# Spreading the last batch's row scatters, fillers, blankings and routing over the blocks of two expert mixtures

## The reference

```python
x = x + 0.5 * ffn(layernorm(x))
x = x + attention(layernorm(x))       # 16 heads of 8, q = k = v
x = x + 0.5 * ffn(layernorm(x))       # the same weights

# ffn: rows are normalised again (gain and bias), a router picks 2 of 8 experts
logits = xf @ router_w
scores, idx = top_k(logits, 2); gate = softmax(scores)
# each expert: layernorm, x1 = x @ W1 + b1 (512 wide), x2 = clip(x @ W2 + b2, -20, 20)
#   hidden = clip(x1 * silu(x2)); y = clip(hidden @ Wo + bo)
out = sum over the experts of gate * y
```

## Time and profile before

| | |
|---|---|
| median of 3 runs | 1469.3 us (1467.14 to 1470.9) |
| profiled execution | 1478.64 us, span 1476.9 us |
| PE busy | 1268.9 us (86%) |
| DVE busy | 1175.9 us (80%) |
| ACT busy | 898.2 us (61%) |
| GpSimd busy | 515.8 us (35%) |
| chain that ended last | PE 52%, DVE 24%, issue 8%, DMA 4%, SyncE's queue 4%, ACT 4% |

### The profile page before, as it was taken

How to read it: one execution, slowest core, us unless ns; L and a number is a source line. 1 busy time by engine, 2 the same in 40 slices (tenths; PEclk the granted TensorE clock), 3 DMA queues, 4 the chain that set the end, 5 groups by cost and what they waited for, 6 DMA issues and landing times.

```text
span 1476.9 us, 29483 instructions
## 1 busy us (share of the span) xinstructions
PE 1268.9 (86%) x10053; PEld 653.3 (44%) x10053; DVE 1175.9 (80%) x2341; ACT 898.2 (61%) x1882; POOL 515.8 (35%) x603
## 2 busy tenths in 40 slices
PE   3735999887789999999969999969996988799992
PEld 3634788775122223323213223213321237688881
DVE  8783888787988998888948898948897648778885
ACT  1212455554368888787748887748875864455651
POOL 3873453343432002324342433330444022433331
PEclk9999999999699999999979999979999999899996
DMA  7124454553302110021111011101100222355635
GB/s 256 41 73 155 163 189 177 223 196 100 86 14 84 35 35 26 11 84 36 27 37 35 22 37 34 42 23 35 35 4 29 78 88 104 119 185 195 237 144 181
DMA packets 65382, 135.58 MB, mean 92 GB/s; under 512 B 13330, under 2 KB 34932, under 8 KB 65204
## 3 DMA queue, kind: packets, MB, share of 16 engines
q1 hardware_dynamic: 56052, 115.39, 22.9%
q0 software_dynamic: 8704, 16.93, 3.4%
q10 hardware_dynamic: 480, 1.38, 0.3%
HBM read 47.35 MB, written 25.07 MB: 49 GB/s over the span
## 4 chain that ended last, share of the span: by engine, by line
PE 52%; DVE 24%; issue 8%; DMA 4%; SPq 4%; ACT 4%; another core or an unknown queue 2%; POOL 2%; ACTq 0%; DVEq 0%; POOLq 0%
PE psum L2188 13%; DVE att_neg_part L1874 10%; PE psum L2164 7%; PE psum L2098 6%; PE psum L2086 5%; PE psum L2088 5%; PE psum L2168 5%; PE psum L2145 5%; DVE stats L1529 2%; DMA ffn_block_rows<-rows_dram 2%; ACT att_probs L1408 1%; DVE att_neg_part L1879 1%; DVE ffn_x2c L1815 1%; DVE ffn_hidden L1826 1%
## 5 line engine op out<-in xcount | busy, mean ns | idle before, releaser
L1408 ACT ACTIVATE att_probs<-psum 128x512 f32<-128x512 f32 x1024 | 556.3, 596 | 171.1 <-PE psum L2170 104.6
L1874 DVE TENSOR_REDUCE att_neg_part<-psum 128x2 f32<-128x1024 f32 x441 | 532.0, 1222 | 91.6 <-PE psum L2146 73.2
L2188 PE MATMUL psum<-att_probs,att_values 128*16 128x256 f32 x4096 | 325.1, 390 | 7.3 <-ACT att_o_t L1423 3.9
L1375 ACT ACTIVATE ffn_silu<-ffn_x2c,ffn_rec 128x256 f32<-128x256 f32 (+1 forms) x320 | 154.6, 487 | 192.7 <-DVE ffn_x2c L1815 141.2
L1237 POOL DMA_INDIRECT y_dram<-ffn_y,ffn_block_rows x144 | 142.2, 988 | 291.1 <-ACT ffn_y L1393 262.9
L2145 PE MATMUL psum<-att_right,att_left 64*128 64x512 bf16 x512 | 200.4, 392 | 44.4 <-ACT att_probs L1408 16.5
L1815 DVE TENSOR_SCALAR ffn_x2c<-psum,ffn_rec 128x256 f32<-128x256 f32 (+1 forms) x320 | 162.5, 513 | 61.1 <-PE psum L2088 40.8
L2167 PE MATMUL psum<-att_right,att_left 64*128 64x512 bf16 x512 | 201.0, 393 | 10.6 <-DVE att_neg_part L1874 8.2
L2164 PE MATMUL psum<-att_right,att_left 64*128 64x512 bf16 x512 | 200.7, 392 | 4.4 <-DVE att_neg_part L1874 4.3
L2146 PE MATMUL psum<-att_right,att_left 64*128 64x512 bf16 x512 | 200.9, 393 | 0.0
L2168 PE MATMUL psum<-att_right,att_left 64*128 64x512 bf16 x512 | 196.1, 383 | 0.0
(11 more groups left out here) (215 smaller groups left out, 1532.3 us busy)
## 6 DMA issues: line engine op xcount, KB each, us to landing
ffn_rec<-record SPq DMA_DIRECT2D x80, 776.5 KB, 3.6
ffn_block_rows<-rows_dram SPq DMA_DIRECT2D x64, 130.0 KB
att_left<-q_parts_dram SPq DMA_DIRECT2D x64, 96.0 KB
att_right<-q_parts_dram SPq DMA_DIRECT2D x124, 48.0 KB
record<-in_L_ffn_W SPq DMA_DIRECT2D x16, 256.0 KB, 6.3
last_y<-y_dram SPq DMA_DIRECT2D x8, 512.0 KB, 7.4
att_right<-q_parts_dram SPq DMA_DIRECT2D x92, 32.0 KB
y_dram<-ffn_y,ffn_block_rows POOLq DMA_INDIRECT x144
```

The lines of the kernel that those rows point to most:

```text
L1408: S.activation(probs[:, slot % PROBS, :], ring_bank(("score", slot))[:, :], ACT.Exp, scale=SCALE).then_inc(att_bank.by_act, 1)
L1874: last = V.tensor_reduce(out=neg_part[:, h % 2, keys, p::PAIR, t], in_=psum[:, low:high + 1, :], axis=AX.X, op=ALU.max, negate=True)
L2188: last = TE.matmul(value_bank[head * VS:head * VS + VW, q], values[:, b % 2, kt, team * TEAM + head, :], probs[:, (UNIT * n + j) % PROBS, ...
```

## The change

In mixture 0 the last batch's 16 scatters go from the end of the first routing into the blocks from 3 on, alternately two and one a block. The blankings go from block 8 to block 14, and memsets are cut: values into one piece per tile, operands into pieces of 256 columns, also for the two sets blanked ahead of attention. The fillers go one a block into blocks 8 to 15 (mixture 0) and two a block into 13 to 16 (mixture 1). In mixture 1 the eight scatters of `JOBS[-2]` are spread over slots 0 to 24, those of `JOBS[-1]` over slots 36 to 52, its other steps over slots 11 to 34 in smaller parts, and the late lay-out into eight parts in slots 35 to 49 with some independent instructions no longer waiting for each other. `JOBS[-1]` becomes a GpSimd job for `xf` and its rows, and its exponential is e to the ratio as a power on GpSimd, for which DVE's gates wait. ACT runs one small Silu before each mixture.

```diff
@@ build_macaron
+    BLANK = 256
         def on_pool(job):
-            return job[0] == 1 and job[1] < B - 1
+            return job[0] == 1 and job != JOBS[-2]
@@ TAIL
-        plan_tail([0], "route", JOBS[-2], ROUTE_STEPS - 1)
+        plan_tail([0, 0, 12, 16, 16, 20, 20, 24], "route", JOBS[-2], ROUTE_STEPS - 1)
...
-        for step, slot in ((0, 10), (1, 12), (2, 14), (3, 15), (5, 17), (6, 19), (7, 20), (8, 21), (9, 23), (10, 24), (11, 25)):
+        plan_tail([11, 13], "route", last_job, 0)
+        for step, slot in ((1, 14), (2, 15), (3, 20), (9, 30), (10, 31)):
             plan_tail([slot], "route", last_job, step)
-        plan_tail([26, 28, 30, 32], "route", last_job, ROUTE_STEPS - 1)
-        plan_tail([27, 29, 31], "lay", 1, 0)
-        BEGIN = 8
+        plan_tail([22, 23], "route", last_job, 5)
+        plan_tail([24, 25, 26, 27], "route", last_job, 6)
+        plan_tail([25, 27, 29, 31], "route", last_job, 7)
+        plan_tail([28, 29], "route", last_job, 8)
+        plan_tail([32, 33, 34], "route", last_job, 11)
+        plan_tail([36, 36, 40, 44, 44, 48, 52, 52], "route", last_job, ROUTE_STEPS - 1)
+        plan_tail(range(35, 51, 2), "lay", 1, 0)
+        BEGIN = 3
@@ HEAD
-        plan_head(BEGIN, [(HC * n, "blank", n, 0) for n in range(6)])
+        for n in range(BT * TOPK):
+            HEAD[HC * (n * 2 // 3)].append(("route", JOBS[B - 1], ROUTE_STEPS - 1, (n, BT * TOPK)))
+        plan_head(BEGIN + 11, [(HC * n, "blank", n, 0) for n in range(6)])
@@ first_routing
-            yield from steps(B - 1, (SCATTER,))
@@ sync_experts
-                sync_fillers(0)
             for i in range(SLOTS[k], EARLY):
                 sync_next_block(k, i)
-                if k == 1 and i == 13:
-                    sync_fillers(1)
+                sync_fillers(k, i)
...
-        def sync_fillers(k):
-            Q.wait_ge(laid_out, 3 * k + 2)
-            for e in range(E):
+        def sync_fillers(k, block):
+            first, some = ((8, 1), (13, 2))[k]
+            few = [e for e in range(E) if first + e // some == block]
+            if few:
+                Q.wait_ge(laid_out, 3 * k + 2)
+            for e in few:
@@ pool_blank_values, pool_blank_operands
-            pool_settle(G.memset(values[:, s, :, :, :], 0.0))
+            for t in range(BT):
+                pool_settle(G.memset(values[:, s, t, :, :], 0.0))
...
-            blank = G.memset(side[s][rows, heads, :], 0.0)
-            if n < 3:
-                pool_settle(blank)
+            for at in range(0, N, BLANK):
+                blank = G.memset(side[s][rows, heads, at:at + BLANK], 0.0)
+                if n < 3 or at + BLANK < N:
+                    pool_settle(blank)
@@ pool_route
+            elif step == 10 and job == JOBS[-1]:
+                G.wait_ge(*by_dve(job, LED))
+                G.tensor_tensor(r.ratio[:, 0:nt], euler[:, 0:1].to_broadcast([P, nt]), r.ratio[:, 0:nt],
+                                ALU.pow).then_inc(last_shared, 1)
@@ scalar_route, scalar_experts
-            elif step == 10:
+            elif step == 10 and job != JOBS[-1]:
...
+            S.activation(warm[:, :], minus_half[:, :], ACT.Silu)
@@ vector_gates
-            V.wait_ge(*by_act(job, SHARED))
+            if job == JOBS[-1]:
+                V.wait_ge(last_shared, 1)
+            else:
+                V.wait_ge(*by_act(job, SHARED))
@@ vector_lay_out_late
-            for at in share(part, 3):
+            for at in share(part, 8):
```

41 lines of the change are left out of this document (26 added, 15 removed).

## The result

The changed kernel takes 1457.4 us (median of 4 runs, 1456.8 to 1460.4) where the kernel before takes 1468.9 (1467.1 to 1470.9): a ratio of 0.9925, with a 95% interval of 0.9906 to 0.9945, or 11.5 us. The forecast was 30, that is 1439.3. The measured 1457.4 lies outside the forecast's own range (1428 to 1450) and just inside the range for 8 in 10 (1426 to 1459), which was made that wide to take in rivals B and C and the bounds of unknown terms. Neither rival came about, so it is luck that this range holds.

A forecast was written before the change was run, and what follows sets the result against it. PE bounds a mixture at 5.62 us a block, so gains lie where PE stops. -12.5 - 5 - 3 + 3 - 12.5 = -30 us takes the median from 1469.3 to 1439.3; own range 1428 to 1450, 8 in 10 1426 to 1459.

The forecast's parts named there:

- B: Mixture 1: GpSimd becomes the bound, so the 12.5 us gain shrinks to 3; total 1449; chance 0.13.
- C: Start of mixture 0: slow stretch is an aftermath of batch 2's scatters and partly stays; loses 12.5, total 1452; chance 0.08.
- Start: Mixture 0's start: spreading the last batch's scatters ends product 0 near 122.5 instead of 135.5; worth 12.5 us (9 to 14).
- Fillers: Mixture 0: eight filler DMAs in one piece delay block 4's rows; one a block hides them, worth 5 us (3 to 5.3).
- rival A: Slow stretches at scatter bursts exist only under the profiler; only 7 us won, total 1462; chance 0.12.
- Blankings: Mixture 0: blanking in pieces, in blocks 14 to 19, keeps DVE's waits inside its slack; worth 3 us (0 to 3.5).
- The pieces ahead of attention: Sets 1 and 2, blanked ahead of attention: eight memsets become 32 with nothing to hide them; costs 3 us (0 to 3.4).
- Mixture 1: Start of mixture 1: excess over full pace falls from 24.2 to 8 + 2 + 1.5 = 11.5; worth 12.5 us (3 to 19).
- the locks: Mixture 1: result scatters and memory locks between DVE and GpSimd add 1.5 us (0 to 4).
- part 1: Mixture 0, blocks 3 to 13: moved scatters fill GpSimd to at most 5.1 of 5.62 us, in an idle gap; worth 12.5.
- rival D: Slowing is spread, not gone: scatters in mixture 0's blocks 3 to 13 cost 41 us more; total 1488; chance 0.07.
- GpSimd's first maxima near 387: Ahead of attention: sign of being right, GpSimd reaching its first maxima near 387, at 383.50 in the kernel before.

The follow-up runs named there:

- before_again: The kernel before, unchanged, run again as a kernel of its own on chip A; ratio 0.9997 to the kernel before at 1476.6 us.
- the four probes: The kernel before with extra row scatters in attention, into tables nobody reads, at various spacings or row sizes; 1427.4, 1422.8, 1429.3 and 1432.7 us on chip B.
- probe_eight: The kernel before plus four bursts of eight row scatters in attention (520, 512, 576, 256 bytes); run twice on chip B, 1429.3 and 1432.7 us.
- after_whole: The changed kernel with operand sets 1 and 2 blanked in whole memsets again; 1466.0 us, 0.9927 of the kernel before (chip A).
- best2: best1 with mixture 0's last-batch scatters held apart, one a block from block 2, behind waits; 1408.5 us, 0.9540 of the kernel before (chip A).
- best1: The changed kernel with sets 1 and 2 blanked in whole memsets and attention's scatters held apart; 1424.5 us, 0.9643 of the kernel before (chip A).
- att_paced: The kernel before with only attention's three bursts of 16 row scatters stretched, 4.4 us apart instead of 1.27; 1438.0 against 1476.8 us, 0.9734 (chip A).

## Why the prediction was wrong

**1. Start: right, a little low.** Forecast product 0 at 122.5 and 12.5 us; it ends at 120.7, 14.8 us earlier (17.7 between before_again and after_whole). Where nothing slows, the kernel before has it at 118.8 to 122.0 (the four probes on chip B), so all of this term was the slow stretch, as forecast.

**2. Fillers: right.** 5.3 and 4.9 us for a forecast of 5. probe_eight adds that the other reading, given with rival A, was wrong, by which the fillers would end in time if nothing slowed: on chip B the burst slows nothing, and eight fillers in one piece still take 9.6 us and still cost 4.6. It is their number, not a slowed queue. So the forecast's price for the case without slowing, 7 us by rival A, and the 7.4 measured on chip B agree by luck: its sum leaves the fillers out.

**3. Blankings: right.** 3.4 us less about 0.6 left in blocks 14 to 20, for a forecast of 3. The pieces ahead of attention: the five traces with them have the 32nd exponential 59.5 to 62.2 us after the last product (mean 61.1), the ones with whole memsets 56.8 to 58.8 (mean 57.7) but for one. That is +3.4 by the mean, for a forecast of +3. Four of the five are from chip B; the one from chip A, 59.5, gives +1.8. The exception is the profiled execution of before, with 60.9; set against it alone, the term seems to be missing. No timed pair shows this term.

**4. Mixture 1: one half right.** Without slowing, blocks 1 to 12 take 80.6 us, 13.2 over full pace; the forecast had 11.5 (8 + 2 + 1.5). On the locks: each of DVE's instructions set against the median of its form, they are there 1.7 us (chip A) to 2.2 us (chip B) longer in all, against 1.5 in the sum; that term was about right. What failed is the sentence "of that some 5.5 are the slow stretch's share: the eight row scatters no longer follow each other". They don't follow each other, they follow result scatters, and the slowing didn't go, it grew. By the difference of the two kinds of chip it costs 87.4 - 80.6 = 6.8 us on chip A after the change, and 91.5 - 87.3 = 4.2 before it.

**5. The failed step** is in part 1: "at most 5.1 of 5.62, in a gap that is idle now", which puts the cost of the moved scatters at nothing, together with what was held against rival D, "batches with pauses between pairs show none of it". Two a block with a pause say nothing of four and then three with 0.3 to 0.8 us between the groups. I had the number that should have warned me, 0.5 us between the groups, and had written the rival's condition as "whatever kind they are"; I gave it 0.07 and priced it at 41 us in mixture 0 alone. Its pattern is what happened, at 12.1 us in mixture 0 (14.6 in blocks 3 to 13 of after_whole) and 2.6 more in mixture 1, where the forecast had 5.5 less: together 20 us, about the 18.5 that are missing. Half the blocks were spared: once blocks have been slowed, GpSimd waits 3.6 to 5.1 us for the next results and starts the next row rested. Of the forecast's own signs of being wrong one came true, "a slow stretch inside blocks 3 to 13 of either mixture".

One sign among those of being right was itself wrong. "GpSimd's first maxima near 387" adds the pieces to 383.50 but leaves out the 20.5 us that the same sum wins in mixture 0 ahead of them; it should have read 366. They came at 375.84, later than that by about the 12.1 us of slow blocks less what the start won beyond its term.

**The sum again**, for the two traces shown: start -14.8, fillers -5.3, blankings -3.4 + 0.6, new slow stretches in mixture 0 +12.1, mixture 1 with its start -7.7. The rest is attention and the ends: -3.4 from block 20 up to the last exponential and +3.5 behind block 12 of mixture 1. Together -18.4; the traced spans differ by 18.3. In the 3.4 the price of the pieces is hidden behind the oddly long stage of the traced before (60.9 instead of 57.6), which explains 3.3 of the 7 us by which the traced difference is larger than the timed one. And 3.7 of the 7.7 are the stretch between the last exponential and the end of mixture 1's product 0, which is 17.1 us in the traced before but 14.2 in before_again and 13.3 in the changed kernel: some 3 us of that are the trace of before too. Had the slowing gone, mixture 0 would have lost 12 to 16 us less (12.1 in the trace, 16.0 by best2) and mixture 1 up to 7 less: an estimate of 24 to 34 us in all, from the 11.5 measured. That sum was not measured on chip A; what was measured there is its larger part, the 16.0 us between best1 and best2.

**The rivals.** A fell with att_paced. The 9.3 us between the profiled execution of before and its median needed no price of profiling: here the profiled executions lie among the others (1474.9 beside a median of 1475.8 for before_again), and the one of before was a long one. The Trainium skill, "Runtime: NRT & Kernel Launch", section "The ~15µs preamble/postamble breakdown", puts a profile's total some 6.2 us above the execution time; no run here shows that gap. B: from product 0 to product 12 of mixture 1 PE waits 0.5 us for GpSimd, and no wait of DVE for GpSimd of that length shows; GpSimd was not the bound. C: product 0 ended at 120.7, no aftermath.

## What to carry to other kernels

When work is moved into a gap, look at what the gap stands next to: an engine's queue with pauses and the same queue without may behave quite differently, and the share of busy time (5.1 of 5.62) doesn't show which one you get. Hold such instructions apart, for instance by a wait for the other engines' progress; here one scatter a block behind such a wait took back 16 us. And take the same kernel's trace twice, on another chip if you can, before a difference of 3 us between two traces is given to the change.

## What the runs showed of the hardware

- **Groups on different chips differ in this by 66 us of 1475.** The same kernel takes 1476 and 1409.5 us, each on at least two chips. The stages of the table say where: the start of mixture 0 (137.4 and 120.6), attention (785 and, in the changed kernel, 743) and mixture 1 (91.6 and 87.3); in all of them scatters stand in a row, and blocks 3 to 20 of the kernel before, which have no such rows, take 104.5 us on both. att_paced and best2 bring chip A to chip B's numbers in attention and mixture 0. What differs between the chips is not known.
- **Count.** On chip A three scatters in a row with 1.7 us of rest lose nothing, and neither does the row of four in mixture 0 of the changed kernel that has 2.45 us of rest behind it (164.99 to 169.8, block 8 at 5.62). Seven within some 9 us, of rows and results mixed, cost 1.4 to 4.8 us, whether the longest pause in them was 0.3 or 0.8 us, and sixteen of rows 13. So results count too: in the row of seven only three were row scatters. That two chips' difference and the count are one mechanism is argued, not shown.
- **The best kernel on chip A is best2**, 68 us under before. On chip B the waits in attention bring nothing: 4 us more in the traces of that stage, 1.2 us more in timed runs, which is within noise.
